# Residual graph layer with layer normalisation: the normalisation's shift computed by GpSimd instead of VectorE

## The reference

```python
# x: 50000 x 512 float32; src, dst: 62500 edges, sorted by dst, one self loop per node among them
msg  = x[src]
agg  = segment_sum(msg, dst, n)
deg  = segment_sum(1, dst, n)
mean = agg / maximum(deg, 1)
h    = mean @ W_l + b + x @ W_r
u    = x + h * sigmoid(h)
out  = (u - mean(u)) / sqrt(var(u) + 1e-5)      # per row of 512
```

## Time and profile before

| | |
|---|---|
| median of 3 runs | 1673.95 us (1671.81 to 1675.46) |
| the profiled execution | 1673.7 us, span 1671.9 us |
| mean granted TensorE clock | 0.990 |
| PE busy | 1602.2 us (96%) |
| DVE busy | 1413.4 us (85%) |
| ACT busy | 1035.4 us (62%) |
| POOL busy | 1015.3 us (61%) |
| DMA moved | 209 GB/s in the mean, 256 GB/s read and written in HBM over the span |

### The profile page before, as it was taken

The page is one execution under the profiler, slowest core; times in us unless marked ns, Lnnn a source line. Parts: engine busy times, 40 slices in busy tenths (PEclk is TensorE's granted clock), DMA queues, the critical chain, the costliest instruction groups (busy, mean ns, idle before and its releaser), DMA issues.

```text
span 1671.9 us, 30356 instructions
## 1 busy us (share of the span) xinstructions
PE 1602.2 (96%) x7886; PEld 1315.8 (79%) x7886; DVE 1413.4 (85%) x2174; ACT 1035.4 (62%) x1433; POOL 1015.3 (61%) x1307
## 2 busy tenths in 40 slices
PE   7998899999999999999999999999999999999995
PEld 5887677777778788888878888887888888888884
DVE  7888899989995888888888888888888888888886
ACT  4443333333334677777767767777777776777775
POOL 6445555555553666666666666666666666666664
PEclk9999999999999999999999999999999999999998
DMA  5445688878884666656666666665666666666664
GB/s 182 148 163 175 190 255 248 254 233 249 254 242 141 197 203 209 227 195 223 202 200 227 197 220 209 211 223 191 211 216 205 226 199 220 208 202 224 199 221 158
DMA packets 204144, 349.26 MB, mean 209 GB/s; under 512 B 37020, under 2 KB 51126, under 8 KB 204117
## 3 DMA queue, kind: packets, MB, share of 16 engines
q1 hardware_dynamic: 156135, 274.22, 49.1%
q0 software_dynamic: 46944, 74.22, 16.6%
q10 hardware_dynamic: 1038, 0.50, 0.1%
HBM read 288.78 MB, written 139.67 MB: 256 GB/s over the span
## 4 chain that ended last, share of the span: by engine, by line
issue 28%; PE 27%; POOL 19%; DVE 12%; ACT 9%; POOLq 2%; DVEq 1%; DMA 1%; SPq 0%; ACTq 0%
PE pH L498 23%; POOL cor L399 6%; ACT O L742 4%; DVE Z L1011 4%; DVE stats L1026 3%; POOL rstd L470 3%; POOL light_cor L399 3%; PE pT L566 2%; POOL l_var_eps L450 2%; ACT cor L696 2%; POOL var_eps L467 2%; ACT light_o L759 2%; DVE l_stats L1053 2%; POOL l_rstd L452 1%; PE pT L507 1%
## 5 line engine op out<-in xcount | busy, mean ns | idle before, releaser
L498 PE MATMUL pH<-ws_hi,x_hi 128*128 128x512 f32 x1564 | 631.5, 404 | 21.2 <-issue 14.6
L498 PE MATMUL pH<-ws_hi,x_lo 128*128 128x512 f32 x1564 | 613.8, 392 | 0.0
L498 PE MATMUL pH<-ws_lo,x_hi 128*128 128x512 f32 x1564 | 611.7, 391 | 0.0
L399 POOL DMA_INDIRECT cor<-correction_rows,node_now x347 | 370.6, 1068 | 215.5 <-POOL node_now L431 148.5
L498 PEld LDWEIGHTS pH<-ws_hi,x_hi 128*128 128x128 f32 x1564 | 295.3, 189 | 85.6 <-issue 30.8
L750 ACT ACTIVATE Z<-Z 128x1024 f32<-128x1024 f32 x174 | 184.2, 1059 | 284.7 <-DVE Z L1011 174.2
L498 PEld LDWEIGHTS pH<-ws_hi,x_lo 128*128 128x128 f32 x1564 | 294.9, 189 | 64.5
L498 PEld LDWEIGHTS pH<-ws_lo,x_hi 128*128 128x128 f32 x1564 | 295.7, 189 | 55.3
L742 ACT ACTIVATE O<-Z,shift,rstd 128x512 f32<-128x512 f32 x347 | 261.4, 801 | 3.7 <-DVE shift L1037 3.7
L1011 DVE TENSOR_TENSOR Z<-pH,cor 128x1024 f32<-128x1024 f32 x174 | 212.0, 1218 | 35.7 <-issue 23.8
L1026 DVE BATCH_NORM_STATS2 stats<-Z 128x6 f32<-128x512 f32 x347 | 221.5, 680 | 0.0
(11 more groups left out here) (134 smaller groups left out, 1834.1 us busy)
## 6 DMA issues: line engine op xcount, KB each, us to landing
X<-in_x SPq DMA_DIRECT2D x173, 512.0 KB
out<-O SPq DMA_DIRECT2D x173, 512.0 KB
correction_rows<-c_out SPq DMA_DIRECT2D x98, 256.0 KB
light_x<-in_x SPq DMA_DIRECT2D x66, 256.0 KB, 2.6
light_h<-early_product SPq DMA_DIRECT2D x44, 256.0 KB
out<-light_o SPq DMA_DIRECT2D x44, 256.0 KB
join_row<-joined SPq DMA_DIRECT2D x98, 64.0 KB
light_h<-in_x SPq DMA_DIRECT2D x22, 256.0 KB, 2.7
```

The costliest lines, as they stand in the source:

```text
L399: g.indirect_dma_start(out=out_, out_offset=None, in_=table, in_offset=bass.IndirectOffsetOnAxis(ap=idx, axis=0), bounds_check=bound, oob_ ...
L498: last = mm(ps, a[:, k], w[:, k], start=(n == 0), stop=(n == len(terms) - 1))
```

## The change

The shift is now computed on POOL, right behind rstd: -mean is made there (`less`, a multiplication by a tile of minus ones) between var + eps and the power, and `shift = less * rstd` behind the power. The same is done for the light tile. DVE's `make_shift` and `light_make_shift` are gone, and so are POOL's waits for them. DVE's moments now wait for the shift of two pairs before (POOL) where they waited for its rstd. One more small memset stands at the start of POOL's queue (`minus_one`), and PE, ACT and DVE wait for 6 constants instead of 5. To make room, `row_ends` of the edge stage uses a part of Z that is idle then.

```diff
@@ POOL: light_make_rstd, make_rstd
                 wait(pool, light_mv, l + 1)
-                wait(pool, light_shift, l)
                 wait(pool, light_normed, l)
                 pool.sem_inc(gate, 1)
                 g.tensor_scalar(l_var_eps[:], l_mv[:, 1:2], EPS, None, ALU.add).then_inc(light_eps, 1)
-                pool.wait_ge(light_eps, l + 1)
+                g.tensor_tensor(l_less[:], l_mv[:, 0:1], minus_one[:, 0:1], ALU.mult).then_inc(light_eps, 1)
+                pool.wait_ge(light_eps, 2 * l + 2)
                 g.tensor_tensor(l_rstd[:], l_var_eps[:], minus_half[:, 0:1], ALU.pow).then_inc(light_rstd, 1)
+                pool.wait_ge(light_rstd, l + 1)
+                g.tensor_tensor(l_shift[:], l_less[:], l_rstd[:], ALU.mult).then_inc(light_shift, 1)
...
                 wait(pool, mv_made, 2 * t + 2)
-                wait(pool, shift_made, t - 1)
                 wait(pool, normed, t - 1)
...
-                pool.wait_ge(eps_added, t + 1)
+                g.tensor_tensor(less[0:rows, b, 0:nt], mv[0:rows, b, 0:nt, 0], minus_one[0:rows, 0:nt], ALU.mult
+                                ).then_inc(eps_added, 1)
+                pool.wait_ge(eps_added, 2 * t + 2)
                 g.tensor_tensor(rstd[0:rows, b, 0:nt], var_eps[0:rows, b, 0:nt], minus_half[0:rows, 0:nt], ALU.pow
                                 ).then_inc(rstd_made, 1)
+                pool.wait_ge(rstd_made, t + 1)
+                g.tensor_tensor(shift[0:rows, b, 0:nt], less[0:rows, b, 0:nt], rstd[0:rows, b, 0:nt], ALU.mult
+                                ).then_inc(shift_made, 1)
@@ DVE: moments; make_shift and light_make_shift and their places in the order
-                wait(dve, rstd_made, t - 1)
+                wait(dve, shift_made, t - 1)
...
-            def make_shift(t, q, u):
-                nt, rows = pair_shape(t)
-                b = u % 2
-                wait(dve, rstd_made, t + 1)
-                wait(dve, normed, t - 1)
-                v.scalar_tensor_tensor(shift[0:rows, b, 0:nt], mv[0:rows, b, 0:nt, 0], -1.0, rstd[0:rows, b, 0:nt],
-                                       ALU.mult, ALU.mult).then_inc(shift_made, 1)
...
                 shifted(t, q, u, -1, NP, residual)
-                shifted(t, q, u, -2, NP, make_shift)
                 light(q, u)
```

More of the change, by code:

```diff
@@ L54, in gnn_layer @@
         zeros = sb("zeros", [P, P], f32)
-        minus_half = sb("minus_half", [P, 2], f32)
+        minus_half, minus_one = sb("minus_half", [P, 2], f32), sb("minus_one", [P, 2], f32)
         bias_rows = sb("bias_rows", [P, D], f32)
@@ L72, in gnn_layer @@
         rstd = sb("rstd", [P, 2, 2], f32)
-        shift = sb("shift", [P, 2, 2], f32)
+        shift, less = sb("shift", [P, 2, 2], f32), sb("less", [P, 2, 2], f32)
         node_idx = sb("node_idx", [P, NTILES + 1], i32)
@@ L80, in gnn_layer @@
         l_now = sb("l_now", [P, 1], i32)
+        l_less = sb("l_less", [P, 1], f32)
         e_x, e_t, e_out = (l_x, l_h), (l_cor, l_z), (l_u, l_o)
@@ L124, in gnn_layer @@
         t_rdeg = sums[:, 0, 3, 0:P]
-        row_ends = sb("row_ends", [1, 3, P], f32)
+        row_ends = Z[0:1, 3, 1, 0:3 * P].rearrange("p (a n) -> p a n", a=3)
         pT = [ctx.enter_context(nc.psum_tensor(f"pT{b}", [P, 2, D], f32)) for b in range(2)]
@@ L372, in _ @@
             g.memset(minus_half[:], -0.5).then_inc(consts, 1)
+            g.memset(minus_one[:], -1.0).then_inc(consts, 1)
             g.memset(dst_f[:, 0:1], -1.0).then_inc(consts, 1)
@@ L489, in _ @@
             mm = nc.tensor.matmul
-            pe.wait_ge(consts, 5)
+            pe.wait_ge(consts, 6)
             def three(ps, hi, lo, w_hi, w_lo, arriving=None):
@@ L704, in _ @@
             act.wait_ge(mask_clear, 1)
-            act.wait_ge(consts, 5)
+            act.wait_ge(consts, 6)
             single(0, expand_mask)
@@ L896, in _ @@
             loop_row(1)
-            dve.wait_ge(consts, 5)
+            dve.wait_ge(consts, 6)
             dve.wait_ge(t_ready, 1)
@@ L1051, in light_moments @@
                 wait(dve, light_u, l + 1)
-                wait(dve, light_rstd, l)
+                wait(dve, light_shift, l)
                 v.bn_stats(l_stats[:], l_u[:]).then_inc(light_stats, 1)
@@ L1056, in light_moments @@
                 v.bn_aggr(l_mv[:], l_stats[:]).then_inc(light_mv, 1)
[L1058 to L1062, removed]
             def light(q, u):
-                if u == 0:
-                    light_at(q - 1, light_make_shift)
                 if u == 1:
@@ L1087, in _ @@
             single(NP - 1, residual)
-            single(NP - 2, make_shift)
             single(NP - 1, moments)
-            light_tail(light, NP, 4 * EARLY)
-            single(NP - 1, make_shift)
-            light_tail(light, 4 * EARLY, 4 * EARLY + 4)
+            light_tail(light, NP, 4 * EARLY + 4)
 _INS = ["x", "src", "dst", "L0_gnn_W_l", "L0_gnn_W_r", "L0_gnn_b"]
```

## The result

The changed kernel takes **1683.39 us** (median of 4 runs, 1683.2 to 1685.05) beside 1674.05 for the kernel before (4 runs, 1671.81 to 1675.46): ratio 1.0063, interval 1.005 to 1.0075. It is slower by 9.3 us, 0.6%, and the whole interval lies above 1. The forecast was 1641 us, with a range of 1633 to 1670 and a chance of 0.81 for faster.

What follows compares the result with a forecast made beforehand. A ring through DVE, ACT and POOL, without PE work, was taken to set the 25.97 us round; cutting POOL's link to DVE would leave PE bounding. Stage -30 and end -3 took 1673.7 to 1641 us, range 1633 to 1670.

Steps and rivals of the forecast that it cites:

- DVE as the link: Node stage: a ring through DVE, ACT and POOL sets the 25.97 us round; DVE is late because it waits for POOL.
- rival 3: PE's lost 0.6 us a round is its own loop closing, DVE's lag only coinciding: about 1666 us, chance 0.06.
- the 0.6: PE, first matmul of one product: 0.61 us lost each round, read as waiting for DVE's x_lo.
- The 34 us that could be gained: Node stage, first to last transposes: 1130.9 us against 1096.8 at PE's pace, so 34.1 to gain at most.
- The products' price: POOL: `less` and `shift` at 0.25 us each plus a 0.08 hop, 2.9 us a round over five groups.
- The rule of twice VectorE's time: Skill page's estimate for POOL's two-operand work: 0.31 us an operation, POOL's round 24.8, still under PE's.
- The end: After PE's last matmul: DVE no longer lags and its rstd waits go, -3 us, between 0 and -5.
- I price stretching at no loss to PE: POOL's operations held up by DVE's residual cost PE nothing; other bound 5.4 us a round.
- the lag frees POOL from the residual: POOL, no longer waited for by DVE, slips later until hits take no more than its 1.2 us spare.
- POOL's sum: POOL's round: 21.26 us without waits and stretching, plus 2.9 added, needs 24.2, 1.2 under PE's.
- the limit: ACT bounds POOL's lag, wanting the shift about 4 to 5 us after the earliest moment; lag stays under it.
- rival 1: POOL's queue becomes the bound and the kernel slower: rounds of 26.8 to 27.71 us, 1709 to 1749; chance 0.14.

Runs made afterwards that it cites:

- e4: Changed kernel with the residual adding a PSUM tile instead of X, so one SBUF input (output not the layer's): 1626.69 us, ratio 0.9735 to the kernel before.
- e6: Changed kernel with var_eps and `less` both made on VectorE, leaving POOL the power and the shift: 1629.4 us, ratio 0.9724 to the kernel before.
- e1: Changed kernel with only `less` moved back to VectorE, for pairs and light tile: 1678.91 us, ratio 1.0048 to the kernel before.
- e11: Repeat, in a later comparison, of the changed kernel with var_eps and `less` both on VectorE: 1627.84 us, ratio 0.9735 to the kernel before.
- e3: Changed kernel with the pairs' shift put back on VectorE, so only the light tile's is made by POOL: 1664.47 us, ratio 0.9957 to the kernel before.
- e9: Changed kernel with var_eps moved to VectorE and `less` kept on POOL: 1645.53 us, ratio 0.984 to the kernel before.

## Why the prediction was wrong

**DVE as the link: right.** The chain lost its DVE part, DVE's waits for POOL are gone, and in e4 and e6, where POOL keeps up, PE's transposes stand 6.33 us apart over the loop's end too, DVE's Z waits for the product, and in e6 PE has no unnamed waits left that the view lists. So rival 3, that the 0.6 is the closing of PE's own loop, is excluded, as it is by the changed kernel, where that step takes 6.33. (The prediction calls it the step in which the hardware loop closes. The loop that closes there is DVE's: its Z at 1020.62 comes 0.59 late with nothing named. PE's own loop closes two steps earlier, in a step of 6.33.) And DVE's waits were worth something by themselves: at 541.47 in the kernel before DVE waits 5.42 us for POOL, and PE's step there takes 11.48; the first 8 steps of the changed kernel take 48.0 us instead of 53.4. After 16 steps 1.9 us of this are left.

```profile
541.47 0.16 DVE L1037 SCALAR_TENSOR_TENSOR shift<-mv,rstd 128x2 f32<-128x2 f32 x1 [5.42 <-POOL rstd L470]
```

The 34 us that could be gained in the stage were there too: e6's stage, from the first to the last transposes, is 1093.0 us against 1130.9.

**The products' price: right, a little high.** `less` takes 0.19 us and an unhit shift 0.19 to 0.20, where 0.25 was taken; with the 0.08 between dependent operations five groups add 5 x (0.19 + 0.20 + 0.08) = 2.35 us a round instead of 2.9. The rule of twice VectorE's time would have been too high as well: 0.20 against 0.16 is 1.25 times. (But POOL needs two such operations, 0.39 us, for the shift that VectorE made in one of 0.16.) That page (the Trainium skill's "GPSIMD Engine Reference", 4.1 Engine selection) was right to speak against the change, but not by this price.

**The end: right.** -3 was taken; what follows the last transposes shrank by 3.0.

**Failed: "I price stretching at no loss to PE", and with it "the lag frees POOL from the residual".** The argument was that a late POOL would settle where the residual doesn't meet it. In the sum it stands as -30 us for the stage; the stage grew by 18.2. The runs showed 3.7 us of stretching a round by the table's count, where 2.6 could fit. Two parts of the argument fell:

- I let only the small operations of a group be hit. The indirect DMAs are hit as well, up to 1.70 for 1.00 (e6), and light_cor 1.83 in the mean (e1) where it takes 1.15 in e4. A DMA of about 1 us stands on POOL nine times a round, so a POOL that is behind has work of that kind under DVE's residual at every lag that e6 passes: 2.7 to 3.5 us a round in e6 from a lag of 7.3 down to 1.5.
- I counted only the residual. The light tile's light_z and light_u have two SBUF inputs too, 0.69 and 0.68 long, and hit l_var_eps and a cor.

The rest of POOL's sum was right. The 1.85 us of hits and the 21.26 without them stand for the round that was read; the table's 2.6 and 20.5 are a wider count, which takes the first DMA's 1.15 against 1.00 for stretching too. By the prediction's own count the round shown of the changed kernel has 2.8 us of hits: 0.97 and 0.69 on two shifts, 0.44 on the light var_eps, 0.47 on light_cor, 0.2 on a cor. So POOL's work is 26.5 - 2.8 = 23.7, where 24.2 was forecast, and the 0.5 between them is the products' price. **The room was 25.36 - 23.7 = 1.6 us a round, more than the 1.2 counted on, and hits of 2.8 came in place of hits that fit into it.**

Once the round is longer than PE's, POOL falls behind until ACT stops it, as the text said of the limit; but ACT isn't a limit at which nothing is lost. Behind its light_o and normalise stand cor and x_hi, then DVE's x_lo, and then PE; DVE's residual comes late with them and meets POOL again. That this last link holds the stretching at its size is argued from the rows: no run cuts it alone.

The bound was in the text: rival 1 came true, in its place (POOL's queue, twice two operations in each group) and its sign, but not by its sum. It gave rounds of 26.8 to 27.7 with products of 0.42 and at most the old stretching of 1.85. With the measured products and that stretching it gives 21.26 + 2.35 + 1.85 = 25.5, which is below the 25.97 of before: by this sum it is the larger stretching, and not the products alone, that made the kernel slower. The time follows from the round: 26.49 - 25.97 = 0.52 over the 39 rounds behind the first 16 steps is 20, and the 1.9 won before them leaves 18 (18.2 measured). With 5.5 less ahead of the stage and 3.0 less behind it that gives 1683.

The place of the trap is the Trainium skill's "SBUF — State Buffer" (SBUF: two separate sides), which was cited for small operations. For two SBUF inputs it speaks of GpSimd operations that read SBUF, and for the making of DMA descriptors it names only DVE's two-port modes; e4 shows by taking the residual's second SBUF input away that the residual does it here: cor's mean goes from 1.091 to 1.063 and light_cor's from 1.610 to 1.149. These DMAs also read their row numbers from SBUF (`node_now`, `l_now`); which part of their making is held up, no run here tells.

## What to carry to other kernels

An operation of 0.2 us that is put on a queue costs what it does to the fill of that queue: add up the engine's work per round, add the stretching, for which every instruction of the queue counts that can meet a two-SBUF-input operation of VectorE (indirect DMAs included), and compare with the round of the engine that is to bound. The stretching of the kernel before is not enough for this sum: it gives 22.8 + 2.6 = 25.4 us here, just at PE's pace, where 26.49 was measured. Over the kernels of this study with the residual as it was it lay between 2.3 and 4.2 us a round, so a queue with less room than that is at risk. Don't let "it will lag into a quiet place" stand as a price: no lag that e6 went through was quiet. And when a wait between two engines is cut, move the work to the side with room: taking the link away gave 9.3 us of loss with all four operations on POOL, and 44.4 us of gain (1672.24 - 1627.84, e11) with two of them on VectorE, where they take 0.16 us each.

## What the runs showed that was not expected

- The same execution can hold two self-sustaining phases: e3's rounds of 26.16 and 25.33 us, changed over by late indirect DMAs of POOL near 1133 and 1439.
- Taking 0.55 us of work from POOL (22.8 to 22.2, e1) gave 0.09 us a round; taking 1.2 (21.6, e9) gave 0.94. The stretching moved from 3.7 to 4.2 and 4.0 in between.
- One operand is worth as much as the better place of the work: the residual with a PSUM input gives 2.4% on the kernel before (e4b), and on the changed one the same time as e6 does, against the kernel before (0.9735; e6 and e11 0.9724 and 0.9735). Whether the layer can be written so that it has one was not tried.
